# Graph layer with residual and layer norm: two native chunks, one joint power, y normalised in place

## What is computed

```python
mask = incidence_m > 0
head = mask.astype(float)
head = head / jnp.maximum(jnp.sqrt(jnp.sum(head * head, axis=-1, keepdims=True)), EPS)
inc = incidence_m + head
edge_fea = inc @ cur
edge_degree = jnp.sum(inc, axis=-1, keepdims=True)
# ... returns edge_fea / edge_degree, and outside:
x = _layernorm(x + _L0_gnn_ref(x, adj), axis=-1)
```

## Time and profile before

| what | value |
|---|---|
| median of 3 runs | 418.78 us (416.98 to 418.84) |
| profiled execution, its own time | 418.74 us |
| its span | 416.9 us |
| PE busy (matmul) | 393.3 us, 94% |
| DVE busy | 378.9 us, 91% |
| ACT busy | 372.4 us, 89% |
| POOL busy | 334.4 us, 80% |
| moved by DMA | 79.94 MB, mean 192 GB/s |
| granted TensorE clock, share of full speed | 0.996 |

### The profile page before, as it was taken

One profiled execution on the slowest core, in us unless ns is written; L12 is line 12 of the kernel. 1 busy time (PEld: TensorE's weight loads), 2 busy tenths in 40 slices (PEclk: granted clock), 3 DMA queues, 4 the chain that ended last, 5 costly groups with the idle time before them and its releaser, 6 DMA issues.

```text
span 416.9 us, 8794 instructions
## 1 busy us (share of the span) xinstructions
PE 393.3 (94%) x2204; PEld 347.5 (83%) x2204; DVE 378.9 (91%) x750; ACT 372.4 (89%) x512; POOL 334.4 (80%) x242
## 2 busy tenths in 40 slices
PE   0788999999899899999999999999999999999994
PEld 0777889888787788888888888888888888888884
DVE  0798898999999999999999999999999999999941
ACT  4975999999899899999999999999999999998420
POOL 2210589898789999999999999999999999999860
PEclk9999999999999999999999999999999999999998
DMA  8999997577647576766676666666666666661100
GB/s 233 262 236 260 261 259 215 178 231 224 206 126 224 162 230 204 211 205 196 209 213 196 207 195 196 199 204 196 206 215 197 206 196 197 196 206 35 38 27 13
DMA packets 36178, 79.94 MB, mean 192 GB/s; under 512 B 9536, under 2 KB 17728, under 8 KB 36160
## 3 DMA queue, kind: packets, MB, share of 16 engines
q1 hardware_dynamic: 35776, 78.68, 64.9%
q10 hardware_dynamic: 384, 1.05, 0.9%
HBM read 75.50 MB, written 4.19 MB: 191 GB/s over the span
## 4 chain that ended last, share of the span: by engine, by line
PE 57%; POOL 13%; issue 7%; DVE 6%; ACT 2%; POOLq 0%; DVEq 0%
PE edge L1132 32%; PE edge L1141 16%; POOL inc_split L516 11%; PE edge L1083 9%; DVE inc L683 3%; DVE incT L699 2%; ACT scaled L245 1%; POOL inc_split L530 1%; POOL rstd L500 1%; POOL norm L496 1%; PE sums L1078 1%; ACT sign_out L234 0%; DVE stats L741 0%; DVE rows L731 0%; DVE rows L736 0%
## 5 line engine op out<-in xcount | busy, mean ns | idle before, releaser
L516 POOL TENSOR_TENSOR inc_split<-incT,inc_split 128x896 fp32r<-128x896 f32 x120 | 252.4, 2129 | 4.2 <-DVE incT L699 4.1
L1132 PE MATMUL edge<-x_split,inc_split 128*128 128x512 f32 (+1 forms) x870 | 208.7, 392 | 0.0
L1132 PEld LDWEIGHTS edge<-x_split,inc_split 128*128 128x128 f32 x870 | 157.1, 188 | 29.9
L683 DVE SCALAR_TENSOR_TENSOR inc<-raw,scaled 128x1024 f32<-128x1024 f32 x128 | 153.4, 1200 | 3.7 <-ACT scaled L245 3.5
L699 DVE STREAM_TRANSPOSE incT<-inc 128x1024 f32<-128x1024 f32 x128 | 155.7, 1227 | 0.4
L245 ACT ACTIVATE scaled<-raw,norm 128x1024 f32<-128x1024 f32 x128 | 141.6, 1109 | 11.2 <-POOL norm L535 4.4
L234 ACT ACTIVATE sign_out<-raw 128x1024 int8<-128x1024 f32 x128 | 133.5, 1043 | 2.0 <-DMA raw<-in_adj_dram 2.0
L1141 PEld LDWEIGHTS edge<-x_split,inc_split 128*128 128x128 f32 x840 | 104.9, 191 | 2.3
L1141 PE MATMUL edge<-x_split,inc_split 128*128 128x256 f32 x840 | 105.9, 283 | 0.0
L256 ACT CAST inc_split<-incT 128x896 fp32r<-128x896 f32 x90 | 81.9, 935 | 6.7 <-DVE incT L699 6.6
L1083 PE MATMUL edge<-x_native,incT 128*128 128x256 f32 x256 | 61.5, 381 | 5.5 <-DVE incT L699 4.8
(11 more groups left out here) (37 smaller groups left out, 137.4 us busy)
## 6 DMA issues: line engine op xcount, KB each, us to landing
raw<-in_adj_dram SPq DMA_DIRECT2D x504, 128.0 KB, 2.5
rows<-in_x_dram SPq DMA_DIRECT2D x32, 128.0 KB, 2.4
out_dram<-rows SPq DMA_DIRECT2D x32, 128.0 KB, 2.1
x_stage<-in_x_dram SPq DMA_DIRECT2D x8, 256.0 KB, 10.5
x_stage<-in_x_dram SPq DMA_DIRECT2D x8, 192.0 KB, 12.2
raw<-in_adj_dram ACTq DMA_DIRECT2D x8, 128.0 KB, 4.9
x_native<-in_x_dram SPq DMA_DIRECT2D x4, 128.0 KB, 6.4
```

Source lines behind the costliest of these rows:

```text
L516: nc.gpsimd.tensor_tensor(lo_of(s, q), incT[:, s, 0:SPLIT, q, :], hi_of(s, q).bitcast(fp32), ALU.subtract).then_inc(lo_by_pool, 1)
L683: nc.vector.scalar_tensor_tensor(inc[:, q, :], raw[:, s, q, :], 0.0, scaled[q % 2][:, :], ALU.is_gt, ALU.add, accum_out=part_sums[:, s, 0, ...
L1132: last = nc.tensor.matmul(edge[s][:, c0:c1], inc_split[s][:, 0, b, :, :].rearrange("p q j -> p (q j)"), x_split[:, b, :, :].rearrange("p h ...
```

## The change

Five things are changed, and the order lists with them.

- NATIVE goes from 4 to 2, so 30 chunks a tile are split; the split quarters have 960 columns, and the pieces of x are 8, 8, 8 and 6 chunks.
- Count and variance lie beside each other (`count_var`), as do norm and rstd (`norm_rstd`). `norm_of(t)` raises all five columns at once, to 0.5 and -0.5: the norm of tile t and the rstd of tile t - 4, and waits for that variance too. `rstd_of` alone is left for the last four tiles.
- `normalise` writes over y; the result slots are gone. The store reads y, and `y_first` waits for the store of the tile two back.
- There is one residual slot; its load is issued one iteration later, behind the store, and waits for the y of the tile before.
- The shift is a tensor_scalar, mean times a pointer to rstd times -1, after the fourth transpose of its iteration. In ACT's loop the normalise comes four instructions later.

In the lists ahead of the loop the same operations stand in another order, on all engines, and more warm-up products are on PE at the start. The small tensors now lie in one (`small`). The core of the diff:

```diff
-    NATIVE = 4
+    NATIVE = 2
     SPLIT = B - NATIVE
...
-        rows = sb("rows", [P, 6, D], fp32)
-        xres = rows[:, 0:2, :]
-        y = rows[:, 2:4, :]
-        result = rows[:, 4:6, :]
+        rows = sb("rows", [P, 3, D], fp32)
+        xres = rows[:, 0, :]
+        y = rows[:, 1:3, :]
...
+        small = sb("small", [P, 68], fp32)
+        part_sums = small[:, 0:16].rearrange("p (s k q) -> p s k q", s=2, k=2)
+
+        count_var = small[:, 16:26].rearrange("p (s k) -> p s k", s=2)
+        norm_rstd = small[:, 26:36].rearrange("p (s k) -> p s k", s=2)
+        powers = small[:, 36:41]
+        count = count_var[:, :, 0:G]
+        norm = norm_rstd[:, :, 0:G]
...
-        X_AT = [0, 8, 14, 22, SPLIT]
+        X_AT = [0, 8, 16, 24, SPLIT]
...
             def load_residual(t, s, reuse):
                 if reuse:
 
-                    sp.wait_ge(y_ready, t - 1)
-                sp.dma_start(xres[:, s, :], x_rows[t]).then_inc(xres_in[s], 16)
+                    sp.wait_ge(y_ready, t)
+                sp.dma_start(xres, x_rows[t]).then_inc(xres_in[s], 16)
 
             def store(t, s):
                 sp.wait_ge(result_ready, t + 1)
-                sp.dma_start(out_rows[t], result[:, s, :]).then_inc(stored[s], 16)
+                sp.dma_start(out_rows[t], y[:, s, :]).then_inc(stored[s], 16)
...
-            load_residual(1, 1, False)
             for k in range(G):
                 load_quarter(3, 1, k, True)
             for t in range(4, 6):
@@ -202,17 +202,18 @@
                     load_quarter(t, t % 2, k, True)
                 if t == 5:
                     store(0, 0)
-                load_residual(t - 2, t % 2, True)
+                load_residual(t - 3, 1 - t % 2, True)
             with sp.Fori(3, PAIRS) as u:
                 for s in range(2):
                     t = 2 * u + s
                     for k in range(G):
                         load_quarter(t, s, k, True)
                     store(t - 5, 1 - s)
-                    load_residual(t - 2, s, True)
-            for s in range(2):
-                load_residual(TILES - 2 + s, s, True)
-            for t in range(TILES - 5, TILES):
+                    load_residual(t - 3, 1 - s, True)
+            for t in range(TILES - 3, TILES):
+                store(t - 2, t % 2)
+                load_residual(t, t % 2, True)
+            for t in range(TILES - 2, TILES):
...
-            def normalise(t, s, u, reuse=True):
+            def normalise(t, s):
                 act.wait_ge(shift_ready, t + 1)
-                if reuse:
-
-                    act.wait_ge(stored[s], 16 * u)
-                nc.scalar.activation(result[:, s, :], y[:, s, :], ACT.Identity, scale=rstd[:, s:s + 1],
+                nc.scalar.activation(y[:, s, :], y[:, s, :], ACT.Identity, scale=norm_rstd[:, s, G:G + 1],
                                      bias=shift[:, s:s + 1]).then_inc(result_ready, 1)
...
             with act.Fori(5, PAIRS - 2) as u:
                 scale_quarter(2 * u, 0, 2)
                 sign_quarter(2 * u + 1, 1, u, 2)
                 sign_quarter(2 * u + 1, 1, u, 3)
                 round_quarter(2 * u, 0, 0)
                 scale_quarter(2 * u, 0, 3)
-                normalise(2 * u - 3, 1, u - 2)
                 sign_quarter(2 * u + 2, 0, u + 1, 0)
                 scale_quarter(2 * u + 1, 1, 0)
                 sign_quarter(2 * u + 2, 0, u + 1, 1)
                 scale_quarter(2 * u + 1, 1, 1)
+                normalise(2 * u - 3, 1)
                 round_quarter(2 * u, 0, 2)
                 round_quarter(2 * u, 0, 3)
                 scale_quarter(2 * u + 1, 1, 2)
@@ -422,11 +420,11 @@
                 sign_quarter(2 * u + 2, 0, u + 1, 3)
                 round_quarter(2 * u + 1, 1, 0)
                 scale_quarter(2 * u + 1, 1, 3)
-                normalise(2 * u - 2, 0, u - 1)
                 sign_quarter(2 * u + 3, 1, u + 1, 0)
                 scale_quarter(2 * u + 2, 0, 0)
                 sign_quarter(2 * u + 3, 1, u + 1, 1)
                 scale_quarter(2 * u + 2, 0, 1)
+                normalise(2 * u - 2, 0)
                 round_quarter(2 * u + 1, 1, 2)
...
-                nc.gpsimd.tensor_tensor(norm[:, s, :], count[:, s, :], half[:, :], ALU.pow).then_inc(norm_ready, 1)
+
+                pool.wait_ge(var_ready, t - 3)
+                nc.gpsimd.tensor_tensor(norm_rstd[:, s, :], count_var[:, s, :], powers[:, :], ALU.pow).then_inc(norm_ready, 1)
 
             def rstd_of(t, s):
                 pool.wait_ge(var_ready, t + 1)
-                nc.gpsimd.tensor_tensor(rstd[:, s:s + 1], var_eps[:, s:s + 1], minus_half[:, :],
+                nc.gpsimd.tensor_tensor(norm_rstd[:, s, G:G + 1], count_var[:, s, G:G + 1], powers[:, G:G + 1],
                                         ALU.pow).then_inc(rstd_ready, 1)
...
                 norm_of(2 * u + 1, 1)
                 low_quarter(2 * u, 0, 0, behind=1)
                 round_quarter(2 * u, 0, 1, own=False)
-                rstd_of(2 * u - 2, 0)
                 low_quarter(2 * u, 0, 1)
                 low_quarter(2 * u, 0, 2)
                 low_quarter(2 * u, 0, 3)
                 norm_of(2 * u + 2, 0)
                 low_quarter(2 * u + 1, 1, 0, behind=1)
                 round_quarter(2 * u + 1, 1, 1, own=False)
-                rstd_of(2 * u - 1, 1)
                 low_quarter(2 * u + 1, 1, 1)
                 low_quarter(2 * u + 1, 1, 2)
                 low_quarter(2 * u + 1, 1, 3)
...
-                dve.wait_ge(result_ready, t - 1)
+                dve.wait_ge(stored[s], 16 * u)
                 after(t, 2)
-                step(nc.vector.scalar_tensor_tensor(y[:, s, :], edge[s][:, D:2 * D], rdeg[:, :], xres[:, s, :],
+                step(nc.vector.scalar_tensor_tensor(y[:, s, :], edge[s][:, D:2 * D], rdeg[:, :], xres,
...
-                nc.vector.tensor_scalar(var_eps[:, s:s + 1], mean_var[:, s, 1:2], EPS, None,
+                nc.vector.tensor_scalar(count_var[:, s, G:G + 1], mean_var[:, s, 1:2], EPS, None,
                                         ALU.add).then_inc(var_ready, 1)
 
-            def shift_of(t, s):
-                dve.wait_ge(rstd_ready, t + 1)
-                nc.vector.scalar_tensor_tensor(shift[:, s:s + 1], mean_var[:, s, 0:1], -1.0, rstd[:, s:s + 1],
-                                               ALU.mult, ALU.mult).then_inc(shift_ready, 1)
+            def shift_of(t, s, alone=0):
+
+                if alone:
+                    dve.wait_ge(rstd_ready, alone)
+                else:
+                    dve.wait_ge(norm_ready, t + 5 - EARLY)
+                nc.vector.tensor_scalar(shift[:, s:s + 1], mean_var[:, s, 0:1], norm_rstd[:, s, G:G + 1], -1.0,
+                                        ALU.mult, ALU.mult).then_inc(shift_ready, 1)
...
             with dve.Fori(5, PAIRS - 2) as u:
                 inc_quarter(2 * u, 0, 0)
                 degree(2 * u - 2, 0)
-                shift_of(2 * u - 3, 1)
                 inc_quarter(2 * u, 0, 1)
                 inverse_degree(2 * u - 2, 0)
                 transpose_quarter(2 * u, 0, 0)
@@ -941,9 +932,9 @@
...
                 transpose_quarter(2 * u, 0, 3)
+                shift_of(2 * u - 3, 1)
                 inc_quarter(2 * u + 1, 1, 0)
                 degree(2 * u - 1, 1)
-                shift_of(2 * u - 2, 0)
...
+            shift_of(28, 0, alone=1)
             degree(30, 0)
-            shift_of(29, 1)
             inverse_degree(30, 0)
             y_first(30, 0, 15)
             y_second(30, 0)
             statistics(30, 0)
             mean_variance(30, 0)
             variance_eps(30, 0)
+            shift_of(29, 1, alone=2)
             degree(31, 1)
-            shift_of(30, 0)
             inverse_degree(31, 1)
             y_first(31, 1, 15)
             y_second(31, 1)
             statistics(31, 1)
             mean_variance(31, 1)
             variance_eps(31, 1)
-            shift_of(31, 1)
+            shift_of(30, 0, alone=3)
+            shift_of(31, 1, alone=4)
...
-            unsplit_chunks(0, 0, 0, 18, {1: lambda: sum_early(1, 3)})
-            unsplit_chunks(1, 1, 0, 4, {2: lambda: sum_degree(0, 0)})
+            warm_up()
+            warm_up()
+            warm_up()
+            warm_up()
+            warm_up()
+            unsplit_chunks(0, 0, 0, 18, {4: lambda: sum_early(1, 3)})
+            unsplit_chunks(1, 1, 0, 2)
             unsplit_chunks(0, 0, 18, B)
-            sum_early(2, 0)
-            unsplit_chunks(1, 1, 4, B, {8: lambda: sum_early(2, 1), 13: lambda: sum_early(2, 2),
-                                        17: lambda: sum_early(2, 3), 22: lambda: sum_early(3, 0),
-                                        29: lambda: sum_early(3, 1), 31: lambda: [sum_degree(1, 1), sum_early(3, 2)]})
-            tile(2, 0, {("hi", 0): lambda: sum_early(3, 3), ("lo", 19): lambda: sum_quadrants(2, 0, early=True)}, first=True)
-            tile(3, 1, {("lo", 4): lambda: sum_quadrants(3, 1, early=True)})
```

(20 more changed lines are left out.)

326 lines of the change are left out of this document (155 added, 171 removed).

## The result

The changed kernel takes 414.00 us (median of 5 runs, 412.91 to 414.78) against 418.84 for the kernel before (5 runs on the same chip, 416.98 to 420.69). The ratio is 0.9881, with an interval of 0.9843 to 0.9919. The forecast was 413.3 in a range of 411.2 to 417.7: size and direction came out. The profiled execution of the changed kernel took 412.91, with a span of 411.1; that of the kernel before took 418.74, with a span of 416.9.

What follows compares the result with a forecast made beforehand. PE was taken to bound the loop at 11.72 us a tile, with DVE slow before it. 4.8 from PE plus 1.2 under ACT's cap, less 0.4 and 0.2, gave 5.4: 418.74 to 413.3 us, range 411.2 to 417.7.

Steps and rivals of the forecast that it cites:

- the new wait: On POOL, the joint power's wait for the variance of the tile four before; priced at 0.
- rival D: The one-element tensor_scalar shift still waits for POOL, so the stops before the loop stay: 416.2 us, chance 0.07.
- The 3.6 of stops in the earlier trace: Before the loop, PE stops three times for a transpose between 85 and 155 us, 3.6 us in all.
- the cap by ACT: ACT's 9.9 us of waiting, less 4.4 for longer roundings, plus 1.6 from PE's lag, limits the gain to 7.1 us.
- 5. y in place: Normalise four instructions later on ACT, shift behind the fourth transpose on DVE: cost 0, at most 0.3 a tile.
- 6. one residual slot: On SP, the residual load follows a store; it fits DVE's y line by 0.1 to 0.3 us, cost 0.
- rival B: In the loop, a late residual landing sets the pace and the kernel gets slower: 420.3 us, chance 0.07.
- step 7: The order lists shift PE's start on tile 2 by at most about 0.5 us either way.
- 8. Tail: At the end, two stores go out 0.6 us apart: +0.2 us for the last landing.
- The 0.4 for small waits in the loop: Taken off the gain for small waits in a loop with two engines at 11.5 us a tile.
- the room: y in place, one residual slot, the joint power and the new order lists together, for 30 split chunks; taken as 0.
- Rival C: The stretch before the loop comes clean and the whole cap is reached: 411.7 us, chance 0.15.

Runs made afterwards that it cites:

- the two runs that move ACT by +0.25 and -0.2: The changed kernel with the normalise split in two of 128 columns, 420.83 us; the changed kernel with the normalise on 16 of 256 columns, 412.52 us.
- The last experiment: The changed kernel with the normalise moved from ACT to DVE, behind the shift, as a 256-column tensor_scalar with two pointers: 444.24 us, ratio 1.0601.

## Why the prediction was right

1. **PE.** Predicted 0.87, 6.98, 3.59 a tile; measured 0.87, 6.97, 3.59. Over 30 split tiles 4.95 instead of 4.8. Right to the hundredth, because all three prices are rows of one engine that never waits in the loop. Of the 4.95 the two chunks are 30 x 0.145 = 4.35; the other 0.6 came with the rest of the change.
2. **ACT.** A rounding was to cost 0.052 more. With 896 columns it takes 930 ns (in the kernel with four native chunks) and 983 with 960: 0.053. The need of 11.52 against PE's 11.56 was right, and the two runs that move ACT by +0.25 and -0.2 show both sides of it.
3. **POOL.** Subtraction 2267 ns against 2.28, joint power 1176 against 1.16, the price of the new wait nothing (in the whole trace no joint power waits for the variance, and the shift waits for a joint power once, 1.3 us).
4. **DVE.** Shift 183 ns against 0.15. The choice between 0.12 and 2.13 was right, and it was the largest single decision. Its other end was far too cheap: rival D gave 416.2, 2.9 over the forecast or 0.15 a tile, since DVE's 11.45 would still fit under 11.56. The run with the two-SBUF form took 453. D did say that the shift holds up the normalise, but its 2.9 us hold next to nothing for that. All of ACT's work stands behind the normalise, and ACT has no time to spare: 1.67 a tile. The size of the gain before the loop was off too: 1.2 was taken, the shift alone gives 3.9. The 3.6 of stops in the earlier trace rows was the right measure of it; the cap by ACT made me take a third.
5. **y in place**, **6. one residual slot**, **7. order lists.** Priced 0, 0 and "at most about 0.5 either way"; together they cost 2.2 with the new lists. In the loop they do cost nothing (the residual waits are 1.0 us in 4, and DVE has 3 of 50 to spare; rival B did not come), and the start of tile 2 moved by -0.34, as step 7 had it. But each step was costed in the loop or at that start, and none in tiles 2 to 10, where most of the cost is. There the order is written out by hand, and with the old lists DVE waits for the store and the residual whose second buffers were taken away.
8. **Tail.** Predicted +0.2, measured +0.11, with the two stores issued 0.7 apart (408.18 and 408.9).

**The sum.** In the profiled executions: 30 x 0.165 = 4.95 by PE, 0.6 by stops gone before the loop, 0.34 at tile 2, -0.1 at the tail: 5.8, where 4.8 + 1.2 - 0.4 - 0.2 = 5.4 was forecast. The 0.4 for small waits in the loop did not come. By the runs the same 5.4 was made of 1.2 for the shift (measured 3.9), 0 for the room (measured +2.2) and 4.2 for the rest (measured 3.2, as the chunks give nothing before the loop). So the total was right with three terms off: a gain of 3.9 taken as 1.2, a cost of 2.2 taken as nothing, and 1.0 too much for the rest. That they cancel to 0.6 is in good part luck, as nothing in the forecast weighed the room against the shift. What wasn't luck is the cap: ACT has no gap left there from 42 us on, as forecast, and whichever edit frees time there, ACT can give back no more than its 4.5 us of waiting, less 1.4 for longer roundings. 154.51 - 151.42 = 3.1 is just that, and PE has 2.4 of it at tile 11. Rival C, the whole cap, did not come: PE's lag behind ACT fell from 2.2 to 0.5, not to 0.3, and tile 11 starts only 2.4 earlier.

The Trainium skill (SBUF — State Buffer, Who interferes with whom) lists tensor_scalar among the DVE operations that can take the pair of ports shared with GpSimd, if their operands meet certain conditions. The last experiment agrees for 256 columns, 1637 ns in the mean against 0.41 us with no subtraction beside it; for one element it doesn't show, at 183 ns. So the rule was right to be weighed, and the row of the variance line was the right one to decide by.

What stays open: what the 2.2 us for the room consist of with the new lists. The kernel with four native chunks has PE waits before the loop for the y line of DVE (1.3 us in two) and ACT waits for loads (1.2 in two); no run took either away. No run has the two chunks with the old slots either, so whether the chunks could have been had without the room's price is not known.

## What to carry to other kernels

A right total doesn't show right terms: here a gain priced at a third and a cost priced at nothing lay in the same stretch and under the same cap, and only runs that take parts out told them apart. An instruction's stall is priced by who waits behind it: the two-SBUF form cost the kernel before nothing in its loop and costs the changed one 1.67 us a tile. And buffers that are taken away must be costed in the tiles where the order is written out by hand, not in the loop alone.

## What the runs showed of the hardware

- A DVE tensor_scalar on one element from SBUF took 183 ns beside POOL's TENSOR_TENSOR, one on 256 columns with two pointers 1637 ns (410 with no subtraction beside it), and the two-input form on one element 1532 ns. So the operation alone doesn't decide; width or the second pointer does too, and which of them no run tells.
- The power on POOL took 550 to 566 ns for one column, 1013 for four and 1176 for five: 0.15 to 0.16 a column.
- An activation over 256 columns took 601 ns, one over 128 took 488, and one over 16 took 398. Splitting one into two cost 0.25 us of a full ACT; cutting fifteen sixteenths of it gave 0.2 by its mean time.
- DVE's load fell by 10 us of 200 in the loop in the kernel with the shift alone, and neither DVE's inc (1200 ns before, 1203 after) nor POOL's subtraction (2129, 2132) became shorter: the waiting was all in that one instruction.
